# All block sums of a feed-forward stage moved to VectorE, and its work lists put in the order in which TensorE reads them

## The reference

```python
h = silu((x @ w1.T) * w1_s) * ((x @ w2.T) * w2_s)   # 256 -> 1024
h = gelu((h @ h1.T) * h1_s)                         # 1024 -> 1024
h = gelu((h @ h2.T) * h2_s)                         # 1024 -> 1024
x = layernorm(x + (h @ w3.T) * w3_s)                # 1024 -> 256
```

## Time and profile before

| | |
|---|---|
| time of the profiled execution | 772.31 us |
| its span, first to last instruction | 770.4 us |
| TensorE busy | 751.6 us, 98% |
| VectorE busy | 604.6 us, 78% |
| ScalarE busy | 431.9 us, 56% |
| GpSimd busy | 272.7 us, 35% |
| mean granted TensorE clock | 0.990 of full speed |

### The profile page before, as it was taken

The page is one execution under the profiler, slowest core; times in us unless marked ns, Lnnn a source line. Parts: engine busy times, 40 slices in busy tenths (PEclk is TensorE's granted clock), DMA queues, the critical chain, the costliest instruction groups (busy, mean ns, idle before and its releaser), DMA issues.

```text
span 770.4 us, 11857 instructions
## 1 busy us (share of the span) xinstructions
PE 751.6 (98%) x3699; PEld 633.7 (82%) x3699; DVE 604.6 (78%) x1292; ACT 431.9 (56%) x843; POOL 272.7 (35%) x294
## 2 busy tenths in 40 slices
PE   8999999999999999999999999899999998999996
PEld 7788988888888888888888887788787986887886
DVE  5789889876898989999676666967966559778566
ACT  6788743334555656555443346455676464656673
POOL 2777243225574747557252230300200203111003
PEclk9999999999999999999999999999999999999998
DMA  8800000004336454351731021144353101263301
GB/s 277 284 1 0 2 1 1 1 26 140 122 124 206 151 183 147 99 197 39 262 111 45 12 69 20 56 126 158 127 169 131 56 1 55 110 209 119 110 1 58
DMA packets 31706, 77.15 MB, mean 100 GB/s; under 512 B 8736, under 2 KB 13472, under 8 KB 27808
## 3 DMA queue, kind: packets, MB, share of 16 engines
q1 hardware_dynamic: 31360, 76.18, 29.3%
q10 hardware_dynamic: 288, 0.26, 0.1%
HBM read 58.08 MB, written 16.78 MB: 97 GB/s over the span
## 4 chain that ended last, share of the span: by engine, by line
PE 78%; DVE 12%; ACT 4%; issue 4%; POOL 1%; DMA 1%; POOLq 0%; DVEq 0%; ACTq 0%
PE bank L1386 15%; PE bank L1270 8%; PE bank L1534 8%; PE bank L1535 8%; PE bank L1364 7%; PE bank L1365 7%; PE bank L1369 7%; PE bank L1385 6%; PE bank L1242 6%; DVE part_r L2033 2%; DVE part_f L2045 2%; DVE part_f L2052 2%; PE bank L1389 2%; ACT hring L1155 2%; DVE part_f L2124 2%
## 5 line engine op out<-in xcount | busy, mean ns | idle before, releaser
L1386 PE MATMUL bank<-wx_both,hx_hi 128*128 128x512 f32 x512 | 191.5, 397 | 0.0
L1534 PE MATMUL bank<-hring,wring 128*128 128x512 f32 x448 | 177.2, 395 | 7.6 <-DVE part_r L2033 5.7
L1535 PE MATMUL bank<-part_r,wring 128*128 128x512 f32 x448 | 176.4, 394 | 0.0
L1000 ACT ACTIVATE hx_hi<-bank 128x512 fp32r<-128x512 f32 x128 | 76.4, 598 | 175.3 <-PE bank L1369 174.1
L716 POOL TENSOR_TENSOR x_tok<-right,x_tok 128x256 f32<-128x256 f32 x128 | 94.7, 740 | 173.6 <-ACT right L1007 168.4
L2033 DVE TENSOR_TENSOR part_r<-part_f,hring 128x512 fp32r<-128x512 f32 x144 | 95.4, 686 | 51.8 <-ACT hring L1155 51.6
L1806 DVE SCALAR_TENSOR_TENSOR hx_lo<-bank,hx_hi 128x512 fp32r<-128x512 f32 x128 | 87.8, 686 | 51.4 <-ACT hx_hi L1000 50.1
L1386 PEld LDWEIGHTS bank<-wx_both,hx_hi 128*128 128x128 f32 x512 | 96.1, 188 | 16.6
L1385 PE MATMUL bank<-wx_both,hx_lo 128*128 128x256 f32 x384 | 108.7, 283 | 0.0
L1534 PEld LDWEIGHTS bank<-hring,wring 128*128 128x128 f32 x448 | 85.2, 190 | 28.3 <-DVE part_r L2033 7.7
L1535 PEld LDWEIGHTS bank<-part_r,wring 128*128 128x128 f32 x448 | 85.3, 190 | 17.6
(11 more groups left out here) (209 smaller groups left out, 1434.6 us busy)
## 6 DMA issues: line engine op xcount, KB each, us to landing
wring<-h_dram SPq DMA_DIRECT2D x28, 1024.0 KB, 4.8
wx_raw<-in_wx SPq DMA_DIRECT2D x16, 512.0 KB, 7.7
raw_quads<-in_wffn SPq DMA_DIRECT2D x16, 512.0 KB, 5.6
h_dram<-sums SPq DMA_DIRECT2D x8, 1024.0 KB, 4.2
h_dram<-raw_quads SPq DMA_DIRECT2D x8, 512.0 KB, 6.5
stage<-in_wffn SPq DMA_DIRECT2D x12, 256.0 KB, 2.7
x_tok<-in_x SPq DMA_DIRECT2D x1, 2048.0 KB, 11.2
h_dram<-raw_quads SPq DMA_DIRECT2D x8, 256.0 KB, 6.7
```

Source lines behind the costliest of these rows:

```text
L1000: act.activation(hx_hi[:, place, c], bank[b][:, :], ACT.Relu).then_inc(s_relu_ok, 1)
L1386: mm = pe.matmul(DBANK[j][:, :].rearrange("p (h d) -> p h d", h=2), hx_hi[:, place, c, a], wo_hl[:, :, c], start=(c == 0), stop=(c == XC - 1))
L1534: pe.matmul(into[:, :], w, b_hi[:, k], start=(k == 0 and i in (0, 1, 3)), stop=False, skip_group_check=True)
L1535: mm = pe.matmul(into[:, :], w, b_lo[:, k], start=False, stop=(k == KH - 1), skip_group_check=True)
```

## The change

- The four `third` sums of each layer leave GpSimd for a new `third_sum` on VectorE, after the low parts of t2.
- In the second gate group the order of VectorE's list becomes: f11's low parts first, t2 and t4 after, and f21's low parts at the end.
- The end of layer 1 (`layer == 0`): ScalarE makes the four high copies of f11 ahead of the four `curved` of f12; VectorE takes each first sum and low part together and leaves the second sums to the end.
- `x_high` and `x_low` of the later groups go behind block 21 and its copies.
- Group 1's rows are normalised and halved before the flag is loaded; its root is taken one unit earlier on GpSimd, its transposes are issued before SyncE's branch, and its words, `x_high` and `x_low` come one or two gate rows earlier.
- p5 waits for `snap` of its own banks, p6 for `block_22`.

```diff
@@ GpSimd
-                    if u == 5 and last:
-                        ln_rstd(s_f_ve, s_f_rstd, 1)
+                    if u >= 5 and last and u < 7:
+                        ln_rstd(s_f_ve, s_f_rstd, u - 4)
...
-                    pool.tensor_tensor(part[at_["f12"]][:, k], part[at_["f22"]][:, k], part[at_["f12"]][:, k], ALU.subtract).then_inc(s_h_t3, 1)
@@ ScalarE, ffn
-                    if q == 0 and m == 6:
+                    if q == 0 and m == 4:
                         x_high(1, xf_hi)
...
+                    if layer == 0:
+                        for m in range(KH):
+                            high(q, i0 + 7, m)
                     for m in range(KH):
-                        if layer == 0:
-                            high(q, i0 + 7, m)
                         curved(q, layer, "f12", m)
                         if layer == 1:
                             high(q, i0 + 7, m)
-                    if q == 0:
-                        x_high(2 + layer, xf_hi)
                     for m in range(KH):
                         if layer == 1:
                             high(q, i0 + 8, m)
                         curved(q, layer, "f21", m)
                         if layer == 0:
                             high(q, i0 + 8, m)
+                    if q == 0:
+                        x_high(2 + layer, xf_hi)
@@ TensorE, waits of a product
                             elif i == 5:
+                                pe.wait_ge(s_h_snap, (q * 2 + layer) * 3 * KH + 8 + m + 1)
+                            else:
                                 pe.wait_ge(s_h_add, (q * 2 + layer) * 3 * KH + 4 + m + 1)
@@ VectorE
+                def third_sum(q, layer, k):
+                    at_ = PARTS[layer]
+                    dve.wait_ge(s_h_sum, summed(q, layer, "t2", k))
+                    dve.tensor_tensor(part[at_["f12"]][:, k], part[at_["f22"]][:, k], part[at_["f12"]][:, k], ALU.subtract).then_inc(s_h_sum, 1)
...
-                        if n == 4:
+                        if n == 3:
                             norm2_words(1)
-                        if n == 6:
+                        if n == 5:
                             x_low(1)
                         if not first and m < KH:
                             first_sum(q, 0, m)
-                            low_part(q, 0, m)
+                            if m > 0:
+                                low_part(q, 0, m - 1)
                         elif not first:
+                            if m == KH:
+                                low_part(q, 0, KH - 1)
                             second_sum(q, 0, m - KH)
-                            fourth_sum(q, 0, m - KH)
-                            low_part(q, 1, m - KH)
+                            if m > KH:
+                                fourth_sum(q, 0, m - KH - 1)
+                    for k in range(KH):
+                        if k == KH - 1:
+                            fourth_sum(q, 0, k)
+                        low_part(q, 1, k)
...
                         for m in range(KH):
                             low_part(q, i0 + 2, m)
+                        for m in range(KH):
+                            third_sum(q, layer, m)
...
+                        if layer == 0:
+                            block_12(q, 0, 0)
+                            for m in range(KH):
+                                if m < KH - 1:
+                                    block_12(q, 0, m + 1)
+                                first_sum(q, 1, m)
+                                low_part(q, i0 + 7, m)
+                            for m in range(KH):
+                                second_sum(q, 1, m)
...
-                        if q == 0:
-                            x_low(g)
                         for m in range(KH):
                             if layer == 0:
                                 fourth_sum(q, 1, m)
                             low_part(q, i0 + 8, m)
+                        if q == 0:
+                            x_low(g)
```

More of the change, by code:

```diff
@@ L293, in decoder_kernel @@
         s_h_sum = sem("h_sum")
-        s_h_t3 = sem("h_t3")
+        s_h_fourth = sem("h_fourth")
         s_w3_mm = sem("w3_mm")
@@ L372, in summed, with fourth_done @@
         def summed(q, layer, name, k):
-            at_ = {"t1": k, "t2": KH + 2 * k, "t4": KH + 2 * k + 1} if layer == 0 else {"t1": 2 * k, "t2": 2 * k + 1, "t4": 2 * KH + k}
-            return (q * 2 + layer) * 3 * KH + at_[name] + 1
+            return (q * 2 + layer) * 3 * KH + {"t1": 0, "t2": KH, "t3": 2 * KH}[name] + k + 1
+        def fourth_done(q, layer, k):
+            return (q * 2 + layer) * KH + k + 1
         def before_product(q, layer, i):
@@ L600, in turn_halves @@
                                             ).then_inc(s_f_turned, 16)
+            turn_halves(1)
+            sp_.wait_ge(s_wide_f, 1)
+            wide = sp_.value_load(wide_flag[0:1, 0:1], min_val=0, max_val=1)
             def store_rows(n):
@@ L609, in _ @@
             with sp_.If(wide < 1):
-                turn_halves(1)
                 for n in range(4, PAIRS * 2 * PRODUCTS):
@@ L639, in _ @@
                 for g in range(G - 1):
-                    turn_halves(g + 1)
+                    if g > 0:
+                        turn_halves(g + 1)
                     for t in range(g * J, g * J + J):
@@ L802, in ffn_wide @@
                     ln_rstd(s_e_ve, s_e_rstd, g + 1)
[L804 to L808, removed]
-                    if layer == 0:
-                        pool.wait_ge(s_f_hf, (q * 2 + 1) * FC + KH + k + 1 + 4)
-                    else:
-                        pool.wait_ge(s_h_act, q * 2 * 16 + 8 + k + 1)
-                    pool.tensor_tensor(part[at_["f12"]][:, k], part[at_["f22"]][:, k], part[at_["f12"]][:, k], ALU.subtract).then_inc(s_h_t3, 1)
             def rows_added(n):
@@ L822, in ffn @@
             def ffn(q):
-                third(q, 0)
                 if q == 0:
@@ L828, in ffn @@
                     ln_rstd(s_e_ve, s_e_rstd, 2)
-                third(q, 1)
                 if q == 0:
@@ L1146, in high @@
                         act.wait_ge(s_e_y, q0 * 2 * J + (stage_no // 2 + 1) * J) if stage_no % 2 else act.wait_ge(s_w3_mm, q0 * 2 + stage_no // 2 + 1)
-                if name in ("t1", "t2", "t4"):
+                if name in ("t1", "t2"):
                     act.wait_ge(s_h_sum, summed(q, layer, name, k))
+                elif name == "t4":
+                    act.wait_ge(s_h_fourth, fourth_done(q, layer, k))
                 elif name == "f12" and layer < 2:
-                    act.wait_ge(s_h_t3, (q * 2 + layer) * KH + k + 1)
+                    act.wait_ge(s_h_sum, summed(q, layer, "t3", k))
                 elif layer == 0:
@@ L1951, in rest @@
                 norm2_halves(1)
+                dve.wait_ge(s_gated_ok, B * E + 4)
+                dve.wait_ge(s_row_ok, B * E + 4)
+                dve.wait_ge(s_wide_f, 1)
+                wide = dve.value_load(wide_flag[0:1, 0:1], min_val=0, max_val=1)
+                dve.wait_ge(s_small_in, 32)
                 def ffn_wide(g, first, last):
@@ L2051, in fourth_sum @@
                         dve.wait_ge(s_h_act, q * 2 * 16 + 12 + k + 1)
-                    dve.tensor_tensor(part[at_["t4"]][:, k], part[at_["f21"]][:, k], part[at_["t2"]][:, k], ALU.subtract).then_inc(s_h_sum, 1)
+                    dve.tensor_tensor(part[at_["t4"]][:, k], part[at_["f21"]][:, k], part[at_["t2"]][:, k], ALU.subtract).then_inc(s_h_fourth, 1)
+                def third_sum(q, layer, k):
+                    at_ = PARTS[layer]
+                    dve.wait_ge(s_h_sum, summed(q, layer, "t2", k))
+                    dve.tensor_tensor(part[at_["f12"]][:, k], part[at_["f22"]][:, k], part[at_["f12"]][:, k], ALU.subtract).then_inc(s_h_sum, 1)
                 def block_11(q, layer, m):
@@ L2167, in ffn @@
                             block_22(q, layer, m)
-                        def behind(m):
-                            if layer == 0:
+                        if layer == 0:
[3 more added lines that the diff above has]
+                                    block_12(q, 0, m + 1)
                                 first_sum(q, 1, m)
                                 low_part(q, i0 + 7, m)
+                            for m in range(KH):
                                 second_sum(q, 1, m)
[L2174 to L2180, removed]
-                        if q == 0:
-                            x_low(g)
+                        else:
+                            block_12(q, 1, 0)
+                            for m in range(1, KH):
+                                block_12(q, 1, m)
+                                low_part(q, i0 + 7, m - 1)
+                            low_part(q, i0 + 7, KH - 1)
                         for m in range(KH):
```

8 lines of the change are left out of this document (removed).

## The result

The changed kernel takes 759.38 us, the median of four runs (759.21 to 760.14), against 772.0 us for the kernel before on the same chip (four runs, 771.43 to 773.2). The ratio is 0.984, with a 95% interval of 0.983 to 0.985: 12.6 us faster. The forecast was 759.0.

The account below looks back on a forecast made before the run. TensorE, busy 98% of the span, bounds the kernel; only its waits can come back. 16.2 us back, less 1.5, 1.6 and 0.15, about 13.0: 759.3 from the profiled 772.31, less 0.29 for the median, 759.0 us; range 755.7 to 762.8.

Parts of the forecast that it names:

- the transposes: Group 1's transposes and words, between the halves and `x_high`: costed at nothing, at 1.7 us if all 10.1 was needed.
- w3: Layer 2 of pair 0, group 3's `x_high` and `x_low` ahead: part three's last low part 0.15 us late.
- block 22: p5's wait for block 22 in the feed-forward stage: moves off it, 0.76 us back.
- Stall A: TensorE's wait for group 1's low rows near 469 us: costs 3.78 us, all taken back, margin 0.1.
- B and its twin: Low-part waits at p1's fourth chunk, pairs 0 and 1: 4.28 and 4.47 us, both gone with their low clock.
- C: Wait before layer 2 of pair 0: not gone, 1.5 us against 1.66 before, released by ScalarE's gelu.
- The new wait at layer 2's p3: Pair 0, t1's fourth low part 1.5 us late: a wait of 1.6 with the longer first matmul.
- rival 1: The new waits in pair 0 pull TensorE's clock down, up to 1.87 us each: 760.9 to 762.7 us; chance 0.10.
- (2): Group 1 stays late, first wait for `xf_lo`: up to 762.8 us; chance 0.07.
- (3): TensorE waits for nothing, the lists running a little quicker than added up: 755.8 us; chance 0.13.
- (4): Third sums on VectorE come out on TensorE one for one, 9.7 us off the gain: 765.5 us; chance 0.04.
- (5): VectorE becomes the bound, its long sums staying long: slower, about 787 us; chance 0.03.

Follow-up runs that it names:

- the version without waits: Changed kernel with each third sum moved behind block 11 of its chunk, instead of all four ahead of the statistics: 756.24 us, ratio 0.980.

## Why the prediction was right

The mechanism held at each large step, and the losses left to TensorE were put at 3.25 us and measured 2.97. Three small terms were off: the transposes, w3 and block 22. The times below are compared after adding the 1.34 us by which the stage began later in the profiled execution.

- **Stall A.** Said: all of it back, with a margin of 0.1. `x_low` was expected to end at 470.84 and ended at 470.89; TensorE, due at 471.00, lost 0.05. The sum was right, but two things inside it were not. `norm2_apply` took 1.88, not 1.38, and the words waited 0.68 for the transposes, which were costed at nothing. Both were absorbed ahead of `x_high`, which had been expected at 466.84 and started at 466.87: as the prediction had it, it stands in ScalarE's list behind silu 4, and that waits until 465.76 for TensorE. The four words were ready only 0.25 to 0.34 before the copies that read them, so that the transposes cost nothing is in part luck. `norm2_apply` runs there beside two of GpSimd's additions (at 456.67 and 457.76); before, behind GpSimd's last work, it took 1.38. The Trainium skill (SBUF — State Buffer, "Who interferes with whom") counts `tensor_scalar` among the instructions that can contend with GpSimd; these rows agree: in the same trace `norm2_apply` of the next group, at 508.34 with GpSimd idle, took 1.37.
- **B and its twin.** Said: the third sums cost VectorE 1.0 each where they were and 0.6 where they are. The sums fell to 0.69, and p1's last low part started at 492.06 against 492.04 expected. The third sums alone end both waits, and the old gate list in the changed kernel does not bring them back. So it was GpSimd's work beside VectorE's that made p1 late. The prediction added up the new list as a whole and did not part the two; the new order has no share that shows.
- **C.** Said: 1.4 late, 1.5 with the longer first matmul, released by ScalarE's gelu. It cost 1.38. The view names no releaser, but the gelu of block 21 at 536.90 ends at 537.57, 0.10 before TensorE's start at 537.67 (537.69 was expected).
- **The new wait at layer 2's p3.** Said: 1.6, released by a low part at 562.3. It cost 1.52, and TensorE started at 562.34.
- **w3.** Said: 0.15 late. It was about 0.05 late, a wait too short for the view of the waits. TensorE's timeline shows it at part three's first use of its fourth low part, which VectorE had ended at 598.42:

```profile
598.53 0.33 PE L1535 MATMUL bank<-wf_hi,hring 128*128 128x256 f32 x1
598.70 0.28 PE L1536 MATMUL bank<-wf_hi,part_r 128*128 128x256 f32 x1
```

  The two starts lie 0.17 apart, where the others of this part lie 0.12 apart. The place was right and the size three times too large.
- **Block 22 at p5.** Said: 0.76 back. With the other parts in place it is 2.5 by the traces; the prediction did not ask what this wait would have cost in the faster kernel.
- **The rivals.** The clock stayed at 1.00 (rival 1), `xf_lo` was in time (2), two waits were left (3). The one-for-one cost (4) and the long sums (5) fell with the means of 0.69. The Trainium skill's advice that handing work of a saturated VectorE to another engine may make sense (Perfetto Trace Analysis, "Optimizing Scalar/DVE Operations") would have left the sums on GpSimd. That costs about 7 us here, which the same passage's remark on the shared port allows for. Rival 3's time, 755.8, is what the version without waits nearly reaches, 756.24.

## What to carry to other kernels

Where two engines slow each other, count a moved instruction at what it costs in both lists: here 0.6 us of work for VectorE bought 1.0 us back. Once TensorE is the bound, add up its lost starts and walk the lists from the stage's start; an engine's regular gap (here 1.31 us a turn) is the place for moved work, and not the chain ahead of it. A change of several parts should be run part by part: this one held a part worth 8 to 9 us, one worth 3, one (the wait of p5) worth about 2, one worth nothing that the times show and one that cost about 2.

## What was not expected of the hardware

An idle time of TensorE does not by itself tell whether its clock falls. In the kernel before, 1.90 us of idle at stall A was followed by matmuls at the lower clock and cost 3.78 in all; the same idle of 1.90, at the same gate row, cost 2.17 in the kernel with the third sums alone, where from the second matmul on the starts were again 0.23 to 0.24 apart. In the changed kernel with the third sums on GpSimd the two pairs differ as well. TensorE's timeline, first pair 0 and then pair 1:

```profile
494.03 0.47 PE L1542 MATMUL bank<-hring,wring 128*128 128x512 f32 x1 [1.85 <-DVE part_r L2041]
...
496.35 0.80 PE L1542 MATMUL bank<-hring,wring 128*128 128x512 f32 x1 [0.46 <-DVE part_r L2041]
...
646.21 0.47 PE L1542 MATMUL bank<-hring,wring 128*128 128x512 f32 x1 [1.86 <-DVE part_r L2041]
...
648.53 0.50 PE L1542 MATMUL bank<-hring,wring 128*128 128x512 f32 x1 [0.47 <-DVE part_r L2041]
```

and the windows around the second wait of each:

```profile
495.00:500.00 5.00, 4.54 (x14) 3.24 (x13) 5.00 (x12) 0.00 (x0) 0.00 (x0) 0.66 0.28 115
...
648.00:653.00 5.00, 4.53 (x21) 3.69 (x21) 4.96 (x15) 0.00 (x0) 0.19 (x1) 1.00 0.09 38
```

The waits are alike to 0.01 us, and the clock fell to 0.66 on the mean in one and stayed at 1.00 in the other. In this stage of these traces the clock fell after each of the four longest idle times (2.41, 2.56, 2.57 and 2.57 us) and after none of 1.48 us or less that stood alone; at 1.85 to 1.90 it did both. What decides there stays open, and with it whether a wait of 1.9 costs 2.2 or 3.8.
